# Attention on 64-row tiles: two heads at a time, scaled fp16 parts made in QKV, wide and narrow pass-one pieces

## The reference, cut to what matters

```python
x = x + 0.5 * ffn(layernorm(x))
x = x + attention(layernorm(x))
x = x + 0.5 * ffn(layernorm(x))

# ffn: W = base + mean(|w - base|) * sign(w - base), for w1, w2, w3
h = silu(x @ W1.T) * (x @ W3.T); out = h @ W2.T        # 512 -> 1792 -> 512
# attention: 32 query heads of 16, 8 key/value heads, 4 queries share one
q, k = rope(q), rope(k)
scores = where(causal, q @ k.T / 16, lowest)           # 1024 x 1024 per head
out = softmax(scores) @ v @ w_dense.T + b_dense
```

## Time and profile before

| | us |
|---|---|
| runs, median (lowest to highest) | 1745.68 (1744.61 to 1749.37) |
| the profiled execution, its own time | 1748.59 |
| its span | 1746.4 |
| TensorE busy | 1601.1 (92%) |
| VectorE busy | 916.0 (52%) |
| ScalarE busy | 649.0 (37%) |
| GpSimd busy | 239.1 (14%) |
| mean granted clock | 0.97 of full |

### The profile page before, as it was taken

The page is one execution under the profiler, slowest core; times in us unless marked ns, Lnnn a source line. Parts: engine busy times, 40 slices in busy tenths (PEclk is TensorE's granted clock), DMA queues, the critical chain, the costliest instruction groups (busy, mean ns, idle before and its releaser), DMA issues.

```text
span 1746.4 us, 27217 instructions
## 1 busy us (share of the span) xinstructions
PE 1601.1 (92%) x9280; PEld 739.6 (42%) x9280; DVE 916.0 (52%) x1622; ACT 649.0 (37%) x919; POOL 239.1 (14%) x349
## 2 busy tenths in 40 slices
PE   1788999999999879999899899999999999999998
PEld 0233444444445534444444444433444444444443
DVE  7887413324137777777677677773243241232212
ACT  4662112211121125676666576667221211212111
POOL 0310000000005542232222232212000000000000
PEclk9899999999999958999999999999999999999999
DMA  9404400000000000000000000000600000000000
GB/s 388 145 0 182 188 0 1 1 0 1 0 0 1 1 31 2 2 2 2 3 2 2 3 2 2 3 2 2 253 1 0 0 25 0 0 24 0 25 0 24
DMA packets 14804, 57.59 MB, mean 33 GB/s; under 512 B 2992, under 2 KB 2992, under 8 KB 14192
## 3 DMA queue, kind: packets, MB, share of 16 engines
q1 hardware_dynamic: 14704, 56.23, 8.3%
HBM read 40.63 MB, written 15.20 MB: 32 GB/s over the span
## 4 chain that ended last, share of the span: by engine, by line
PE 78%; DVE 13%; issue 4%; ACT 3%; DMA 1%; POOL 1%; SPq 0%; DVEq 0%; ACTq 0%; POOLq 0%
PE ps L1239 30%; PE ps L1260 14%; PE ps L1429 7%; PE ps L1473 7%; PE ps L1455 6%; DVE rowmax L1135 4%; PE ps L1544 3%; PE ps L1342 3%; PE ps L1286 2%; PE ps L1374 2%; PE ps L1432 2%; DMA w_raw<-w1t 1%; ACT qa L726 1%; PE ps L1233 1%; PE ps L1480 1%
## 5 line engine op out<-in xcount | busy, mean ns | idle before, releaser
L1135 DVE TENSOR_REDUCE rowmax<-ps 128x1 f32<-128x512 f32 (+3 forms) x608 | 381.4, 658 | 133.5 <-PE ps L1429 74.9
L768 ACT ACTIVATE probs<-ps 128x1024 f32<-128x1024 f32 (+3 forms) x384 | 292.5, 812 | 171.7 <-PE ps L1455 171.5
L1239 PE MATMUL ps<-xt_hi,w_all 128*128 128x512 f16 x896 | 282.4, 388 | 42.8 <-DVE w_all L925 19.8
L1429 PE MATMUL ps<-ka,qa 96*128 96x512 bf16 (+3 forms) x768 | 243.9, 348 | 38.7 <-DVE rowmax L1135 34.3
L1455 PE MATMUL ps<-qa,ka 99*128 99x512 bf16 (+3 forms) x768 | 190.2, 331 | 9.2 <-issue 7.2
L1013 DVE SCALAR_TENSOR_TENSOR hb<-ps,scal,silub 128x512 f32<-128x512 f32 x56 | 42.0, 750 | 266.6 <-PE ps L1239 266.6
L1239 PE MATMUL ps<-xt_lo,w_all 128*128 128x512 f16 x448 | 174.1, 389 | 0.0
L1473 PE MATMUL ps<-probs,vs 128*32 128x512 f32 (+3 forms) x1536 | 164.1, 499 | 2.4 <-ACT probs L768 1.5
L1429 PEld LDWEIGHTS ps<-ka,qa 96*128 96x128 bf16 x768 | 75.2, 99 | 190.9 <-DVE rowmax L1135 154.6
L1239 PEld LDWEIGHTS ps<-xt_hi,w_all 128*128 (+1 forms) x896 | 89.4, 100 | 156.5 <-issue 45.8
L1239 PE MATMUL ps<-xt_hi,w13b_all 128*128 128x512 f16 x448 | 138.0, 379 | 0.8 <-DVE x L1213 0.8
(11 more groups left out here) (140 smaller groups left out, 1999.7 us busy)
## 6 DMA issues: line engine op xcount, KB each, us to landing
spill<-w_all SPq DMA_DIRECT2D x1, 10752.0 KB, 28.7
w13b_all<-spill SPq DMA_DIRECT2D x1, 7168.0 KB, 19.8
x<-x_in SPq DMA_DIRECT2D x4, 1024.0 KB, 5.3
y_out<-x SPq DMA_DIRECT2D x4, 1024.0 KB, 4.3
wbase<-m1t SPq DMA_DIRECT2D x4, 896.0 KB, 12.5
w_raw<-w1t SPq DMA_DIRECT2D x4, 896.0 KB, 14.1
wbase<-m3t SPq DMA_DIRECT2D x4, 896.0 KB, 23.8
w_raw<-w3t SPq DMA_DIRECT2D x4, 896.0 KB, 24.1
```

The source lines that it names most:

```text
L768: nc.scalar.activation(probs[u % PBUF][:, 2 * pair:2 * pair + 2, 0:q1 - q0], ps[:, 2 * pair:2 * pair + 2, 0:q1 - q0], ACT.Exp, scale=SM_SC ...
L1135: nc.vector.tensor_reduce(dst, ps[:, PASS1 + r % 2, 0:w * len(heads)].rearrange("p (h w) -> p h w", w=w), AX.X, ALU.max).then_inc(p1_read, 1)
L1239: last = mm(ps[:, bank, :], w[a][:, k, bass.ts(t, P)], xt[b][:, k, :], start=(k == 0 and n == 0), stop=(k == HB - 1 and n == 2))
L1429: last = mm(ps[:, PASS1 + r % 2, n * w:(n + 1) * w], qa[v][0:ROWS, h, qt * P:(qt + 1) * P], ka[v][0:ROWS, k0:k0 + w], start=True, stop=not ...
```

## The change

What it does:

- q and k become two fp16 parts, scaled by a power of two that is worked out from the weights' and the bias's bound (into the cosine and sine tables, and out again in the exponential's scale). Slots are high, high, low for q and high, low, high for k: 48 rows of contraction, 50 with two rows of rowmax.
- The parts are made in QKV, tile by tile (`high_parts` on ScalarE, `low_parts` on VectorE), for all groups, into `parts_q` and `parts_k` with 64 columns a head. The splitting on GpSimd and the repeating on ScalarE in attention go.
- One transpose of q serves two heads (`o` 0, 1), the third is k, put twice, at partitions 0 and 64. So two heads of a group stand on partitions 0 to 63 and 64 to 127, and score products of the two contract over different row halves. Three copies a group instead of five, all on ScalarE, as is the copy of the rowmax.
- Pass one has 12 "pair" pieces, two heads into banks 4 and 5 with one reduce over both, and 14 narrow pieces into bank 6. Bank 6 also serves the transposes of q, k, rowmax and context; its uses have turns (`TURN`) and one semaphore `single_taken`. The value products move to bank 7.
- The mask is now added by two products over 64 rows (`lower` 128 columns, `upper` 64 columns).
- The rowmax has two parts and goes to its rows by four DMAs. The row maxima have two buffers.
- Norms 4, 5, 6 are made in the last chunk of FFN1 at its tiles 4, 8, 12, in buffers of their own; norm 7 stays in QKV. VectorE does the cosine of all tiles; GpSimd the sine.
- No hardware loop in attention. The weights for FFN2 come back in another split, w1 as soon as the parts are no longer read.

By `piece_slots` the pieces (w wide, n narrow) and the shared use behind them fall on the slots so: 0: w n n, rowmax; 1: w n n; 2: w n w, q; 3: n w (ahead of the unit's scores); 4: n w, context; 5: n w; 6: none, q; 7: n w n; 8: w n w, context; 9: n w n; 10: w, k; 11: n.

The diff, cut to its core:

```diff
-ROWS = 6 * HEAD
-MROWS = ROWS + 3
+QC, KC = KV_HEADS * QW, KV_HEADS * HEAD
+ROT = QC + KC
+QKV = ROT + KC
+ROWS = 3 * HEAD
+MROWS = ROWS + 2
+M_UNIT = 2.0 ** 15
...
+    double, single = [], []
+    for qt in (7, 6, 5, 4):
+        double += [("pair", [(qt, qt, j, 0, 512)]) for j in (0, 1)]
+    double += [("pair", [(6, 10, j, 512, 384)]) for j in (0, 1)]
+    double += [("pair", [(2, 2, j, 0, 384)]) for j in (0, 1)]
+    for b in (0, 1):
+        single += [(b, [(7, 11, j, 512, 512)]) for j in (0, 1)]
+    for b in (0, 1):
+        single += [(b, [(5, 9, j, 512, 256) for j in (0, 1)])]
+    for b in (0, 1):
+        single += [(b, [(3, 3, j, 0, 512)]) for j in (0, 1)]
+    for b in (0, 1):
+        single += [(b, [(0, 0, 0, 0, 128), (0, 0, 1, 0, 128), (4, 8, 0, 512, 128), (4, 8, 1, 512, 128)])]
+        single += [(b, [(1, 1, j, 0, 256) for j in (0, 1)])]
...
+SHARED = {0: ("rowmax", 0), 2: ("qk", 0), 4: ("ctx", 1), 6: ("qk", 1), 8: ("ctx", 0), 10: ("qk", 2)}
+def shared_use(k, s):
+
+    use = SHARED.get(s)
+    if use is None:
         return None
-    return unit_at(k, s - 1, second, tail)
-
-
-def pair_of(k):
-
-    i, c = k
-    return (c // 2 if i is None else i * (BUF // 2) + c // 2), c % 2
-
-
-def never(k, least=0):
-
-    return k[0] is None and k[1] < least
+    what, n = use
+    g = {"qk": k + 1, "rowmax": k - 1, "ctx": k - 1 - n}[what]
+    return (what, g, n) if 0 <= g < GROUPS else None
...
+    PAIR_BANK, SINGLE_BANK, CTX_BANK = 4, 6, 7
...
+        for g in range(GROUPS):
+            sp.wait_ge(single_taken, taken(("rowmax", g, 0)))
+            for n in range(4):
+                i, b = divmod(n, 2)
+                at_row = 64 * b + ROWS + i
+                sp.dma_start(qa[g % BUF][at_row:at_row + 1, :, :], mrow[4 * i + 2 * b:4 * i + 2 * b + 2, :])\
                     .then_inc(m_placed, 16)
...
+        def high_parts(i):
+            act.wait_ge(sum_ready, i + 1)
+            r = rot[i % 2][:, :].rearrange("p (h d) -> p h d", d=HEAD)
+            nq = KV_HEADS * Q_PER_KV
+            nc.scalar.copy(parts_q[:, i, :, 0:2 * HEAD].rearrange("p h (s d) -> p h s d", d=HEAD),
+                           r[:, 0:nq, :].unsqueeze(2).to_broadcast([P, nq, 2, HEAD])).then_inc(qkhi_ready, 1)
+            nc.scalar.copy(parts_k[:, i, :, 0:ROWS].rearrange("p h (s d) -> p h s d", d=HEAD)[:, :, 0:3:2, :],
+                           r[:, nq:, :].unsqueeze(2).to_broadcast([P, KV_HEADS, 2, HEAD])).then_inc(qkhi_ready, 1)
...
+                if (f, c) == (0, CHUNKS - 1):
+                    for t in range(2, IT):
+                        if t + 2 in LN_AT:
+                            norm_stats(LN_AT[t + 2])
+                        if t + 1 in LN_AT:
+                            normalised(LN_AT[t + 1])
+                        if t in LN_AT:
+                            for j in range(TPC):
+                                ln_lo(LN_AT[t], j)
+                        product(T0 + t, t % 2, bufs)
+                        h_lo(T0 + t, t % 2, bufs)
+                    continue
...
+                    chain(nc.vector.tensor_reduce(bqmax[:, :], bq[:, :], AX.X, ALU.max, apply_absolute_value=True))
+                    chain(nc.vector.tensor_scalar(wc[:, 4, 0:1], allr[:, 3, 1:2], float(HID), bqmax[:, :], ALU.mult,
+                                                  ALU.add))
+                    chain(nc.vector.tensor_scalar(wc[:, 4, 1:2], wc[:, 4, 0:1], 6.0, None, ALU.mult))
+                    power_of_two(4)
+                    for t in (cos, sin):
+                        t2 = t[:, :, :].rearrange("p a b -> p (a b)")
+                        chain(nc.vector.tensor_scalar(t2, t2, wc[:, 4, 3:4], None, ALU.mult))
+                    chain(nc.vector.tensor_scalar(wc[:, 4, 5:6], wc[:, 4, 4:5], SM_SCALE, None, ALU.mult))
+                    chain(nc.vector.tensor_tensor(out=es[:, :], in0=wc[:, 4, 5:6], in1=wc[:, 4, 4:5], op=ALU.mult))
...
+        def low_parts(i):
+            dve.wait_ge(qkhi_ready, 2 * (i + 1))
+            r = rot[i % 2][:, :].rearrange("p (h d) -> p h d", d=HEAD)
+            nq = KV_HEADS * Q_PER_KV
+            nc.vector.tensor_tensor(out=parts_q[:, i, :, 2 * HEAD:ROWS], in0=r[:, 0:nq, :],
+                                    in1=parts_q[:, i, :, 0:HEAD], op=ALU.subtract).then_inc(qklo_ready, 1)
+            nc.vector.tensor_tensor(out=parts_k[:, i, :, HEAD:2 * HEAD], in0=r[:, nq:, :],
+                                    in1=parts_k[:, i, :, 0:HEAD], op=ALU.subtract).then_inc(qklo_ready, 1)
...
+            if kind == "pair":
+                n = k * NPAIR + PAIR_PIECES.index(r)
+                qt, slot, j, k0, w = parts[0]
+                dve.wait_ge(pair_full, n + 1)
+                nc.vector.tensor_reduce(rowmax[:, slot, :, j], ps[:, PAIR_BANK:PAIR_BANK + 2, 0:w], AX.X,
+                                        ALU.max).then_inc(pair_taken, 1)
+                return
...
+        def single_free(use):
+
+            if TURN[use]:
+                pe.wait_ge(single_taken, TURN[use])
...
+        def partial(bank, off, b, v, qt, j, k0, w):
+
+            return mm(ps[:, bank, off:off + w], qa[v][64 * b:64 * b + ROWS, j, qt * P:(qt + 1) * P],
+                      ka[v][64 * b:64 * b + ROWS, k0:k0 + w], start=True, stop=k0 + w < P * (qt + 1))
+
+        def lower(bank, off, b):
+            return mm(ps[:, bank, off:off + P], shifted[64 * b:64 * b + 64, 64:192], negmask[64 * b:64 * b + 64, :],
+                      start=False, stop=False)
+
+        def upper(bank, off, b):
+            return mm(ps[:, bank, off + 64:off + P], shifted[64 * b:64 * b + 64, 0:128],
+                      negmask[64 * b:64 * b + 64, 0:64], start=False, stop=True)
 
         def score_piece(k, r):
 
-            qt, k0, w, heads = PIECES[r]
-            v = buf(k)
-            if r >= 2 or not never(k, 1):
-                pe.wait_ge(p1_read, num(k) * NP_ + (r - 1))
+            kind, parts = PIECES[r]
+            v = k % BUF
             if r == 0:
-                pe.wait_ge(qkt_act, num(k) * 4 + 4)
-                pe.wait_ge(qkt_dve, num(k) + 1)
-            diagonal = k0 + w == P * (qt + 1)
-            for n, h in enumerate(heads):
-                last = mm(ps[:, PASS1 + r % 2, n * w:(n + 1) * w], qa[v][0:ROWS, h, qt * P:(qt + 1) * P],
-                          ka[v][0:ROWS, k0:k0 + w], start=True, stop=not diagonal)
-                if diagonal:
-                    last = mm(ps[:, PASS1 + r % 2, (n + 1) * w - P:(n + 1) * w], ident16[:, :], negmask[:, :],
-                              start=False, stop=True)
-            last.then_inc(p1_full, 1)
+                pe.wait_ge(single_taken, taken(("qk", k, 2)))
+            if kind == "pair":
+                n = k * NPAIR + PAIR_PIECES.index(r)
+                if n:
+                    pe.wait_ge(pair_taken, n)
+                qt, slot, j, k0, w = parts[0]
+                for b in (0, 1):
+                    last = partial(PAIR_BANK + b, 0, b, v, qt, j, k0, w)
+                if k0 + w == P * (qt + 1):
+                    for b in (0, 1):
+                        lower(PAIR_BANK + b, w - P, b)
+                    for b in (0, 1):
+                        last = upper(PAIR_BANK + b, w - P, b)
+                last.then_inc(pair_full, 1)
+                return
+            single_free(("piece", k, r))
+            off = 0
+            for qt, slot, j, k0, w in parts:
+                last = partial(SINGLE_BANK, off, kind, v, qt, j, k0, w)
+                if k0 + w == P * (qt + 1):
+                    lower(SINGLE_BANK, off + w - P, kind)
+                    last = upper(SINGLE_BANK, off + w - P, kind)
+                off += w
+            last.then_inc(single_full, 1)
...
+            for b in (0, 1):
+                last = mm(ps[:, 2 * pair + b, 0:q1 - q0], ka[v][64 * b:64 * b + MROWS, kt * P:(kt + 1) * P],
+                          qa[v][64 * b:64 * b + MROWS, pair, q0:q1], start=True, stop=True)
```

More of the change, by code:

```diff
@@ new lines, in single_bank_uses, with unit_at @@
+def single_bank_uses():
+    out = [("qk", 0, o) for o in range(3)]
+    for k in range(GROUPS + 2):
+        for s in range(NU):
+            if k < GROUPS:
+                out += [("piece", k, r) for r in SLOTS[s] if r not in PAIR_PIECES]
+            use = shared_use(k, s)
+            if use:
+                out.append(use)
+    return {use: n for n, use in enumerate(out)}
+TURN = single_bank_uses()
+def unit_at(k, s):
+    g, u = (k - 2, NU - TAILS + s) if s < TAILS else (k - 1, s - TAILS)
+    return (g, u) if 0 <= g < GROUPS else None
@@ L803, in take_ctx_t @@
+                use = shared_use(k, s)
+                if use and use[0] == "qk":
+                    take_qk(use[1], use[2])
+                elif use and use[0] == "rowmax":
+                    take_rowmax(use[1])
         def take_ctx_t(i):
@@ L1156, in take_rowmax @@
[L1156 to L1168 removed]
+                dve.wait_ge(turned_ready, 2 * (i - 1))
@@ L1190, in body @@
-            if first:
-                split_rowmax(k)
```

(10 more changed lines are left out.)

751 lines of the change are left out of this document (310 added, 441 removed).

## The result

The changed kernel takes 1812.3 us (median of four runs, 1810.7 to 1813.3) against 1746.3 us: a ratio of 1.037, 95% interval 1.036 to 1.038. It is slower by 66 us. The prediction was 1738 us, range 1690 to 1790: wrong in sign and outside the range.

What follows compares the result with a forecast made beforehand. TensorE's queue, one list in program order, was taken as the bound. FFN1 with QKV -8, body 0 -2, fifteen bodies +5 and tail -3 gave -8 us, from 1745.7 to 1738 us, range 1690 to 1790.

Steps and rivals of the forecast that it cites:

- a body of 36.8 us at full clock: Attention: 27.8 us of TensorE's work and 9.0 of waits a body, 1.0 more than before; chance 0.42.
- The layout of the waits: Attention: one body laid out slot by slot, with TensorE waiting 9.0 us for turns of banks, against 4.3 before.
- clock 1.00 in attention: Attention: TensorE's granted clock was to stay at full; below 0.9 would show the prediction wrong.
- rival 2: Attention: waits lower the clock for a third of the time, 4 us a body, 60 in all: 1798 us; chance 0.12.
- TensorE's work, 27.8 us: Attention: products, masks and transposes 27.0 us a body plus 0.8 for tile mode changes, 3.7 less than before.
- Rival 3: Attention: products in different row halves don't overlap, 4.8 us a body, 72 in all: 1810 us; chance 0.06.
- Rival 1: Attention: waits overlap better than laid out, some 6 us, so a body takes 34: 1695 us; chance 0.30.
- Rival 4: Attention: the turns of banks cost more than laid out, a body takes 38.5 us: 1763 us; chance 0.10.
- 4.0 a tile: QKV: 4.0 us a tile (3.9 to 4.5), from TensorE's 3.9 and VectorE's 3.7, 64 us without the norm.
- FFN1, +4: FFN1: with layer norms 5 and 6 moved in, QKV's first product goes from 527 to 531 us.
- Body 0, -2: First attention body, pass one alone: fewer, wider reduces save 3 to 4 us, copies give half back; -6 to +3.
- Tail, -3: Attention's end, pass two alone: score pairs at half the time, ScalarE's 1.94 us a unit becomes the limit; -6 to 0.

Runs made afterwards that it cites:

- e1_fill: The changed kernel with 16 extra pairs of pass-two score products a body, computed in TensorE's waits and overwritten later: 1763.6 us, ratio 1.009.
- e5: e3_rot3 with all score products and masks read from the first row half, so that pairs can't overlap: 1870 us (1845 to 1913), ratio 1.061.
- e11: The kernel before the change, with score products of both passes contracting over 48 rows instead of 96 and 99: 2135 us (2078 to 2184), ratio 1.196.
- e2_hoist: The changed kernel with score pairs moved ahead of the pieces that wait, no work added: 1819.6 us, ratio 1.042.
- e3_rot3: The changed kernel with banks 4, 5, 6 used in rotation, every wide piece as two narrow ones: 1688.0 us, ratio 0.966.
- e8_rot_qkv: e3_rot3 with, in QKV, bias and cosine ahead of low parts, GpSimd's constant fills later and first operand copies ahead of high parts: 1673.3 us, ratio 0.957.

## Why the prediction was wrong, point by point

- **The likeliest case, a body of 36.8 us at full clock.** The layout of the waits held slot by slot: TensorE's idle time in slot 0 is 1.40 and 0.87 us (forecast 1.1 and 0.9), 1.10 in slot 3 (1.1), 0.78 in slot 7 (0.95), 0.95 in slot 11 (1.1), all in all 100.5 us in 13 bodies, 7.7 each against 9.0 (the five largest groups below):

```profile
PE ps L1363 <- ACT qa L679: 24.5, 26, 1.1
PE ps L1363 <- DVE rowmax L1113: 18.1, 13, 1.4
PE ps L1363 <- DVE context L1144: 17.1, 26, 0.8
PE ps L1363 <- ACT ka L679: 12.3, 13, 0.9
PE ps L1409 <- DVE rowmax L1113: 12.2, 14, 0.9
```

- **The step that failed is "clock 1.00 in attention".** The waits were priced once, as time, and the clock was put at full. The bodies ran at 0.85, and that is paid on top: 39.6 us a body, against 36.3 with 4.4 us of idle products put in (e1_fill) and 36.4 (546.6 / 15) in the forecast. That is rival 2, which I gave 0.12 and 1798 us; its 4 us a body above the forecast were measured as 3.2. The forecast is 72 us short in span; the bodies make 47 of them and QKV 20. That the time lies above rival 2's 1798 comes from QKV. The counterargument, that the tail ran at 1.00 on ScalarE's pace, was too thin: the tail has no wait above 0.8 us in TensorE's queue and no narrow piece. But it isn't explained away either: in the tail after, TensorE is busy 25.2 of 34.6 us, less than in a body, at a clock of 1.00. What in a body brings the clock down, the length of single waits, their places or the half-used rows between them, stays open. What I didn't see at all is that with half-used rows the clock falls though TensorE doesn't wait (e5, e11). The Trainium skill, "TensorE: Matmul & The Clock Gate", Part 1, tells of a kernel whose short pauses between groups of matmuls, as it cycles through PSUM banks, let the clock swing. e1_fill (0.85 to 0.98 over the bodies) agrees, the tail and e2_hoist show that it isn't the sum of the pauses alone, and this warning deserved more than 0.12.
- **TensorE's work, 27.8 us.** 28.1 busy in e3_rot3, at full clock. That it fits is in part luck: narrow products overlap with their neighbours (I had counted none), so other terms are too low by as much; which, is open.
- **Rival 3 (row tiles don't overlap)** is refuted: pairs span 0.39 us. **Rival 1** (waits overlap better) did not come true in the changed kernel; with a third bank in rotation the body takes 31.6 us, less than its 34. **Rival 4**: the turns cost 7.7 us, not more than laid out.
- **QKV, "4.0 a tile".** The sum of VectorE's work was about right (3.9 us), the dependence was missed: ScalarE's high parts of 1.42 us stand between sum and low parts with nothing of VectorE's beside them, which gives 5.09 us. Another 5.4 us are a wait for GpSimd, whose constant fills stand ahead of the first sine. The trace shows the fills only from 535.66 to 536.69 and the sine from 543.96, so what holds GpSimd between them isn't seen; with the fills moved back (e8_rot_qkv) the sine starts at 534.96 and this wait is gone. Forecast -12 for the stage, measured +8. e8_rot_qkv, which mends the ring, the fills and the first copy together, gets 14 of these 20 us back; the rest is open.

```profile
545.74 0.83 DVE L1060 TENSOR_TENSOR rot<-rot,rot_s 128x640 f32<-128x640 f32 x1 [5.43 <-POOL rot_s L497]
```

- **FFN1, +4**: +3, right. **Body 0, -2**: 0; VectorE is busy 25.1 us instead of 27.8, but TensorE waits 4.9 us for narrow reduces between pieces and 3.3 for operand copies; with three banks in rotation it takes 29.4 us. **Tail, -3**: 0, though TensorE is busy 25.2 us there instead of 29.4: of its waits 5.6 us end on ScalarE's exponentials, and ScalarE is busy 26.1 us as it was 25.7.
